# Attention over 32 groups of four heads: another order of the step, one call for the values, finished batches at fixed steps, and a prologue by batch

## What is computed

```python
def _L0_xattn_ref(x, ctx, pos_map, ctx_pos_map, Wq, Wkv, Wout, bout):   # 32 heads of 8, 256 keys
    q = (x @ Wq).reshape(b, n, N_HEADS, HEAD_DIM)
    k, v = jnp.split(ctx @ Wkv, 2, axis=-1)
    ...
    q = apply_axial_rope(q, pos_map)
    k = apply_axial_rope(k, ctx_pos_map)
    logits = jnp.einsum('bqhd,bkhd->bhqk', q, k) * scale
    w = jax.nn.softmax(logits, axis=-1)
    attn = jnp.einsum('bhqk,bkhd->bqhd', w, v)
    return attn.reshape(b, n, N_HEADS * HEAD_DIM) @ Wout + bout
x = x + jnp.tanh(g_xattn[0]) * _L0_xattn_ref(_layernorm(x, axis=-1), ctx_1024, ...)
x = x + jnp.tanh(g_ffn[0]) * _L0_ffn_ref(_layernorm(x, axis=-1), ...)   # 2 shared, 32 routed experts, top 6
```

## Time and profile before

| | us |
|---|---|
| median of three runs | 469.26 (468.69 to 469.92) |
| profiled execution | 466.33 |
| its span, first to last instruction | 464.5 |
| TensorE (PE) matmuls busy | 446.4 (96%) |
| VectorE (DVE) busy | 285.4 (61%) |
| ScalarE (ACT) busy | 198.8 (43%) |
| GpSimd (POOL) busy | 141.5 (30%) |
| first score matmul of the loop | at 37.75 |
| transposition with the maxima of the last group | at 178.14 |

### The profile page before, as it was taken

The page is one execution under the profiler, slowest core; times in us unless marked ns, Lnnn a source line. Parts: engine busy times, 40 slices in busy tenths (PEclk is TensorE's granted clock), DMA queues, the critical chain, the costliest instruction groups (busy, mean ns, idle before and its releaser), DMA issues.

```text
span 464.5 us, 8154 instructions
## 1 busy us (share of the span) xinstructions
PE 446.4 (96%) x2515; PEld 334.4 (72%) x2515; DVE 285.4 (61%) x579; ACT 198.8 (43%) x366; POOL 141.5 (30%) x229
## 2 busy tenths in 40 slices
PE   5888999999999998999999999999999999999996
PEld 5556666666666665676887888888888888888885
DVE  7798877777777674554427555554445555544555
ACT  1487887777777655463213222222222222222221
POOL 9066700000000000334245443333444433344430
PEclk9899999999999999999999999999999999999999
DMA  8201111111111000956998332324332233333102
GB/s 225 61 9 50 35 30 33 35 33 33 31 33 36 25 1 0 325 176 176 313 303 210 93 90 90 90 93 115 103 96 91 90 90 90 98 114 104 46 0 92
DMA packets 34056, 43.62 MB, mean 94 GB/s; under 512 B 5633, under 2 KB 28209, under 8 KB 34033
## 3 DMA queue, kind: packets, MB, share of 16 engines
q1 hardware_dynamic: 30737, 42.07, 31.5%
q10 hardware_dynamic: 3296, 1.25, 1.2%
HBM read 37.93 MB, written 1.18 MB: 84 GB/s over the span
## 4 chain that ended last, share of the span: by engine, by line
PE 86%; DVE 5%; DMA 3%; ACT 2%; issue 1%; SPq 1%; POOL 0%; DVEq 0%; ACTq 0%
PE psum L1159 26%; PE psum L1142 25%; PE psum L993 8%; PE psum L1006 7%; PE psum L969 6%; PE psum L956 3%; PE psum L980 2%; DMA G<-gates_by_expert 2%; PE psum L1055 2%; PE psum L912 2%; PE psum L884 1%; PE psum L921 1%; DVE nmax L735 1%; PE psum L1017 1%; SPq L307 1%
## 5 line engine op out<-in xcount | busy, mean ns | idle before, releaser
L608 ACT ACTIVATE hh<-hu 128x512 fp32r<-128x512 f32 x88 | 55.6, 633 | 186.9 <-DVE hu L853 186.9
L853 DVE SCALAR_TENSOR_TENSOR hu<-psum,b1cols,G 128x512 f32<-128x512 f32 x88 | 65.8, 750 | 109.3 <-PE psum L1142 98.9
L735 DVE TENSOR_REDUCE nmax<-psum 128x2 f32<-128x512 f32 x128 | 85.1, 687 | 26.0 <-PE psum L969 24.5
L499 ACT ACTIVATE probs<-psum 128x512 f32<-128x512 f32 x128 | 69.4, 595 | 14.1 <-PE psum L993 13.7
L1159 PE MATMUL psum<-hh,w2h 128*128 128x512 f32 (+1 forms) x188 | 73.5, 391 | 0.4 <-POOL hl L384 0.3
L1159 PE MATMUL psum<-hh,w2l 128*128 128x512 f32 (+1 forms) x188 | 73.2, 389 | 0.0
L1159 PE MATMUL psum<-hl,w2h 128*128 128x512 f32 (+1 forms) x188 | 73.2, 389 | 0.0
L859 DVE SCALAR_TENSOR_TENSOR hl<-hu,hh 128x512 fp32r<-128x512 f32 x88 | 61.4, 700 | 9.6 <-ACT hh L608 9.6
L1142 PE MATMUL psum<-xTh,w1h 128*128 128x512 f32 (+1 forms) x188 | 58.2, 391 | 0.0
L415 POOL CAST w2h<-w 128x256 fp32r x44 | 18.4, 417 | 130.2 <-PE psum L1159 130.2
L1142 PE MATMUL psum<-xTl,w1h 128*128 128x512 f32 (+1 forms) x188 | 57.9, 389 | 0.0
(11 more groups left out here) (150 smaller groups left out, 540.5 us busy)
## 6 DMA issues: line engine op xcount, KB each, us to landing
G<-gates_by_expert SPq DMA_DIRECT2D x40, 256.0 KB, 3.9
w<-in_L_ffn_rw_dram SPq DMA_DIRECT2D x4, 1408.0 KB, 11.9
w<-in_L_ffn_rw_dram SPq DMA_DIRECT2D x2, 2816.0 KB, 17.1
G<-gates_by_expert SPq DMA_DIRECT2D x8, 448.0 KB, 3.6
Kd<-QK SPq DMA_DIRECT2D x104, 32.0 KB, 1.8
G<-gates_by_expert SPq DMA_DIRECT2D x8, 384.0 KB, 3.5
G<-gates_by_expert SPq DMA_DIRECT2D x8, 320.0 KB, 3.7
G<-gates_by_expert SPq DMA_DIRECT2D x8, 192.0 KB, 3.8
```

Source lines behind the costliest of these rows:

```text
L499: act.activation(probs[g % 2][:, kt, 2 * hp:2 * hp + 2, :], ST_BANK[(4 * g + n) % 3][:, :].rearrange("p (h q) -> p h q", h=2), ACT.Exp, sc ...
L608: act.activation(hh[(SHT + j) % 2][:, cols], hu[2 * j + half][:, :], ACT.Relu).then_inc(rhh_ok, 1)
L735: dve.tensor_reduce(nmax[i % 2][:, qt, 2 * hp:2 * hp + 2], S_BANK[n % 2][:, :].rearrange("p (h k) -> p h k", h=2), AX.X, ALU.max, negate=T ...
L853: dve.scalar_tensor_tensor(out=hu[2 * (j % 2) + half][:, :], in0=H_BANK[2 * (j % 2) + half], scalar=b1cols[:, bass.ds(it * len(G) + j, 1)] ...
```

## The change

The loop's step has another order: scores 2, transposition with the maxima, scores 3, values of both halves in one call, finished batches, outputs, score 0 of the next group, shifted scores 0 and 1, next score 1, shifted 2, transposes of the group four ahead, shifted 3. On ScalarE the four exponentials come last in a step; several waits go, since others imply them. Finished batches are handled in fixed steps: transposed in 11, 19 and 27, projected and added in 12, 20 and 28; the copies of the transposed attention go to two tiles of Vx (0 and 3). In the prologue context and rows are loaded and transposed by batch, the statistics of the first two batches go ahead of the others, ScalarE normalises the rows and clears four of the five key buffers, the angle chain on VectorE uses operations with two tensor inputs (against tiles of constants), and the square root is a power of -0.5 on GpSimd, with the Newton step behind it as before. `WARM_UP` and `WARM_START` are 7 and 2 instead of 14 and 8. The shared experts' weights are loaded from SP's queue.

The diff, cut to what the prediction speaks of:

```diff
-WARM_UP, WARM_START = 14, 8
+WARM_UP, WARM_START = 7, 2
...
-        ATTN_STEPS = [GROUPS - 5, GROUPS - 3, GROUPS - 1]
-        PROJ_STEPS = [GROUPS - 4, GROUPS - 2, GROUPS - 1]
-        RESIDUAL_STEPS = [GROUPS - 4, GROUPS - 2, GROUPS - 1]
+        ATTN_STEPS = [NG * (b + 1) + 3 for b in range(B - 1)]
+        PROJ_STEPS = [n + 1 for n in ATTN_STEPS]
+        RESIDUAL_STEPS = PROJ_STEPS
...
+            load_context(0)
+            load_rows(0)
+            sp.dma_start(wkv_sb[:, :], wkv).then_inc(wkv_ld, 16)
+            load_context(1)
+            load_rows(1)
             sp.dma_start(wq_sb[:, :, :], wq.rearrange("(k p) n -> p k n", p=P)).then_inc(wq_ld, 16)
-            sp.dma_start(wkv_sb[:, :], wkv).then_inc(wkv_ld, 16)
+            load_context(2)
+            load_context(3)
+            load_rows(2)
+            load_rows(3)
...
-            for i in range(RING - 1):
-                last = pool.memset(Kd[i][:, :, :].bitcast(F32), 0.0)
-            last.then_inc(kd_clear, 1)
+            then(pool.memset(halves[:, :], -0.5))
+
+            def inverse_root(n, tiles):
+                pool.wait_ge(var_ok, n)
+                pool.tensor_tensor(rough[:, tiles], veps[:, tiles], halves[:, tiles], ALU.pow).then_inc(root_ok, 1)
...
+            def clear_keys(i):
+                if i == 0:
+                    act.wait_ge(consts_ok, 1)
+                act.activation(Kd[i][:, :, :], consts[:, 0, 0:1].unsqueeze(2).to_broadcast([P, GH, N]), ACT.Copy).then_inc(kd_clear, 1)
...
-            square_root(1, slice(0, NT))
-
+            clear_keys(0)
+            clear_keys(1)
+            context(0)
+            context(1)
+            act.wait_ge(ang_ok, 1)
+            act.activation(trig[:, :, :, :], ang[:, :, :].rearrange("p s (t f) -> p s t f", f=4), ACT.Sin).then_inc(trig_ok, 1)
...
+            act.wait_ge(rstd_ok, 1)
+            normalise_rows(0, xn[:, 0], xn_ok)
             read_values(0)
+            evacuate(0)
+            context(2)
+            context(3)
+            act.wait_ge(rstd_ok, 2)
+            normalise_rows(1, xn[:, 1], xn_ok)
             read_values(1)
-            evacuate(0)
             evacuate(1)
-
-            for k in range(KD):
-                act.dma_start(w1s[:, k, :].rearrange("p (e h) -> p e h", h=HID),
-                              sw1.rearrange("e (k p) h -> p k e h", p=P)[:, k]).then_inc(ws_ld, 16)
-            sflat2 = sw2.rearrange("e h n -> (e h) n")
-            act.dma_start(w2s[:, 0:SFULL, :], sflat2[0:SFULL * P, :].rearrange("(t p) n -> p t n", p=P)).then_inc(ws_ld, 16)
-            act.dma_start(w2s[0:SREST, SFULL, :], sflat2[SFULL * P:NS * HID, :]).then_inc(ws_ld, 16)
+            clear_keys(2)
+            clear_keys(3)
...
+                if b + 2 < B:
+                    act.wait_ge(rstd_ok, 3)
+                    normalise_rows(b + 2, xn[:, b + 2], xn_ok)
...
-                    exponentials(g, 0)
-                    exponentials(g, 1)
                 p = (i - 3) // 2
                 if i % 2 and 0 <= p < PAIRS:
-                    act.wait_ge(pv_mm, 2 * (i - 1))
-                    if p >= 2:
-                        act.wait_ge(ot_mm, p - 1)
+                    act.wait_ge(pv_mm, i - 1)
                     act.activation(oT[p % 2][:, :], O_BANK[:, 0:N], ACT.Copy).then_inc(o_ok, 1)
-                if i in ATTN_STEPS[1:]:
+                if i in ATTN_STEPS:
                     transposed_attention(ATTN_STEPS.index(i))
                 if 0 <= g < GROUPS:
-                    exponentials(g, 2)
-                    exponentials(g, 3)
-                if i == ATTN_STEPS[0]:
-                    transposed_attention(0)
...
-            square_root(2, slice(0, NT - TB))
...
-            square_root(3, slice(NT - TB, NT))
...
-            dve.tensor_scalar(sine[:, :, :, 0], pos_sb[:, :, :], 1.0, None, ALU.mult)
-            then(dve.tensor_scalar(sine[:, :, :, 1], pos_sb[:, :, :], FREQ1, None, ALU.mult))
-            then(dve.tensor_scalar(ang[:, 1], ang[:, 0], float(np.pi / 2), None, ALU.add))
-            then(dve.tensor_scalar(turns[:, :, :], ang[:, :, :], float(1 / TWO_PI), ROUND, ALU.mult, ALU.add))
-            then(dve.tensor_scalar(turns[:, :, :], turns[:, :, :], ROUND, None, ALU.subtract))
+            zeros = consts[:, 0].rearrange("p (t a f) -> p t a f", t=NT, a=2)
+            both = [consts[:, n].rearrange("p (s t) -> p s t", s=2) for n in range(4)]
+            for f, factor in enumerate((1.0, FREQ1)):
+                ins = dve.scalar_tensor_tensor(out=sine[:, :, :, f], in0=pos_sb[:, :, :], scalar=factor,
+                                               in1=zeros[:, :, :, f], op0=ALU.mult, op1=ALU.add)
+            then(ins)
+            then(dve.scalar_tensor_tensor(out=ang[:, 1], in0=ang[:, 0], scalar=float(np.pi / 2), in1=both[0][:, 0],
+                                          op0=ALU.add, op1=ALU.add))
+            then(dve.scalar_tensor_tensor(out=turns[:, :, :], in0=ang[:, :, :], scalar=float(1 / TWO_PI), in1=both[1],
+                                          op0=ALU.mult, op1=ALU.add))
...
-                then(dve.reciprocal(rstd[:, rows], root[:, rows]))
-                then(dve.tensor_tensor(newton[:, rows], rstd[:, rows], rstd[:, rows], ALU.mult))
+                then(dve.tensor_tensor(newton[:, rows], rough[:, rows], rough[:, rows], ALU.mult))
...
-            inverse_deviations(0, NT)
-            for b in range(B):
-                normalise_rows(b, xn[:, b], xn_ok)
+            row_variances(0, TB)
+            row_variances(TB, TB)
+            row_scales(0, TB)
+            row_scales(TB, TB)
...
                 multiply_turns(b, 1, A_KV[b % 2][:, :, 0:D])
+                if b == 0:
+                    row_variances(2 * TB, 2 * TB)
+                    add_turns(b, 1)
                 dve.wait_ge(q_mm, b + 1)
                 multiply_turns(b, 0, A_Q[b % 2].rearrange("p (t n) -> p t n", t=TB))
+                if b == 0:
+                    row_scales(2 * TB, 2 * TB)
+                if b:
+                    add_turns(b, 1)
+                add_turns(b, 0)
                 if b == B - 1:
 
                     dve.wait_ge(b1_mm, 1)
                     dve.tensor_copy(b1cols[:, :], A_B1[:, 0:TILES]).then_inc(b1_ok, 1)
                     dve.tensor_scalar(b1half[:, :], A_B1[:, SB_ROW:TILES], 1.0 / NS, None, ALU.mult).then_inc(b1_ok, 1)
-                add_turns(b, 1)
-                add_turns(b, 0)
 
 
             def row_max(i, n):
...
-                dve.tensor_copy(dst[:, :, :, R_MAX], nmax[g % 2][:, :, :]).then_inc(mhi_ok, 1)
+                dve.tensor_tensor(dst[:, :, :, R_MAX], nmax[g % 2][:, :, :],
+                                  consts[:, 0, 0:TB * GH].rearrange("p (t h) -> p t h", t=TB), ALU.add).then_inc(mhi_ok, 1)
...
+                    row_max(i, 3)
+                    maxima(i)
                 if i >= 4 and i % 2 == 0:
                     normalise((i - 4) // 2)
-                if i < GROUPS:
-                    row_max(i, 3)
-                    maxima(i)
                 if i in RESIDUAL_STEPS:
                     residual(RESIDUAL_STEPS.index(i))
...
-            def values(i, kt):
+            def values(i):
 
 
                 b, g = i // NG, i % NG
-                pe.wait_ge(exp_ok, 4 * i + 2 * (kt + 1))
                 second = i % 2
-                if kt == 0 and not second and i:
-                    pe.wait_ge(o_ok, i // 2)
-                for h in range(GH):
-                    ins = pe.matmul(O_BANK[HR * h:HR * h + HR, 0:N], Vx[:, TB * b + kt, GH * g + h, :], probs[i % 2][:, kt, h, :],
-                                    start=(kt == 0 and not second), stop=(kt == TB - 1 and bool(second)),
-                                    skip_group_check=True)
+                for kt in range(TB):
+                    pe.wait_ge(exp_ok, 4 * i + 2 * (kt + 1))
+                    for h in range(GH):
+                        ins = pe.matmul(O_BANK[HR * h:HR * h + HR, 0:N], Vx[:, TB * b + kt, GH * g + h, :], probs[i % 2][:, kt, h, :],
+                                        start=(kt == 0 and not second), stop=(kt == TB - 1 and bool(second)),
+                                        skip_group_check=True)
                 ins.then_inc(pv_mm, 1)
...
+                    keys_copied(0)
                     scores(i, 0)
                     scores(i, 1)
-                if weighted:
-                    values(i - 2, 0)
+                    transposes(AHEAD)
+                    keys_copied(1)
+                if new:
+                    scores(i, 2)
                 if shifted:
                     transposed_with_max(i - 1)
-                if i + AHEAD < GROUPS:
-                    transposes(i + AHEAD)
-                elif i == ATTN_STEPS[1]:
-                    attention_transposed(1)
-                elif i == PROJ_STEPS[1]:
-                    output_projection(1)
-                elif i == ATTN_STEPS[2]:
-                    attention_transposed(2)
                 if new:
```

(27 more changed lines are left out.)

167 lines of the change are left out of this document (103 added, 64 removed).

## The result

The changed kernel takes 456.94 us (median, 456.44 to 457.92), the kernel before 469.25 (468.69 to 469.92): a ratio of 0.9742, 95% interval 0.9723 to 0.9761. 456.2 was forecast. Its profiled run took 456.51 us with a span of 454.7.

A forecast was written before the change was run, and what follows sets the result against it. TensorE was taken to bound the loop, VectorE the part before it. Prologue -6.0, loop -7.0 and tail -0.1 sum to -13.1 us: 453.2 from the profiled run, 456.2 against the median; range 449 to 464.5.

The forecast's parts named there:

- Angle chain, first scores: Prologue: angle chain ends at 6.2 instead of 11.6, first scores move from 37.75 to about 31.8, -6.0 us.
- The power on GpSimd: Prologue and tail: taken at 0.3 us, replacing a square root and reciprocal; over 1 us was a sign of being wrong.
- Steady step: Attention loop: one visit fewer takes TensorE's step from 4.18 to 3.83 us, with bounds 3.77 and 4.1.
- The price of a visit: Attention loop, TensorE: going to the 32-column shape and back costs 0.3 us; two a step become one.
- QT's wait: Attention step, TensorE: 0.06 us lost before the shifted scores, which wait for QT; forecast to go.
- Finished batches: Steps 11-12, 19-20, 27-28: transposes, projection and residual cost 3.9 us each, 11.7 for three, VectorE waits included.
- case 4: Rival, more than forecast: batches cost only TensorE's 2.5 us each, or VectorE's other pre-loop waits go too: 450; chance 0.14.
- Tail: After the loop: values' new place +0.3 us, an exponential table load gone; -0.1 us in all.
- From the profiled run to the median: Whole kernel: 453.2 us from the profiled run; the old median's 2.9 above its profiled run carried over, giving 456.2.
- 1: Rival, loop gives nothing: ScalarE's ring or VectorE's maxima set the step at 4.05 us; time 463.1, chance 0.2.
- 3: Rival, slower: ScalarE's exponentials without overlap make the step 4.5 us on the mean; time 477 us, chance 0.04.
- 2: Rival, prologue gives little (-3 us), since ScalarE took over 7.5 us of clears and normalisations: time 459.2, chance 0.12.

The follow-up runs named there:

- e7: Changed kernel with the four key buffers cleared by GpSimd again, ahead of its halves and first powers, not by ScalarE: 3.7 us more than the changed kernel.
- e4: Changed kernel with the old numbers of warm-up transposes, 14 and 8 in place of 7 and 2: 458.61 us.
- e9: e8 with TensorE's wait for the second group's copied keys moved from ahead of the first group's third scores to behind its fourth: 453.81 us.
- e15: e9 with ScalarE's two gate activations and the table load ahead of them moved behind the last high parts of the prologue: 455.20 us.
- e1: Changed kernel with a group's values in two calls again, the second after the next group's first scores: 468.56 us.
- e5: Kernel before, with the first half of the values moved right ahead of the second half, in the old order of the step: 468.68 us.
- e8: Changed kernel with VectorE's residual ahead of the normalisation and a batch's two statistics behind the next group's first two row maxima: 453.00 us.
- e6: Changed kernel with both the old one-input angle chain and the key-buffer clears on GpSimd: 7.1 us more than the changed kernel.
- e2: Changed kernel with the old angle chain of one-input operations in place of two-input ones: 2.7 us more than the changed kernel.
- e14: e5 with the next group's first scores also moved ahead of the last shifted pair, parting the two score matmuls: 471.44 us.
- e3: Changed kernel with the finished batches at steps 26, 28 and 30 in place of 11, 19 and 27: 454.60 us.

## Why the prediction was right

The time is 0.7 us from the forecast. The parts, as forecast and as the profile has them:

- **Angle chain, first scores.** 6.2 forecast, 5.67 measured; 31.8 and 31.51, so -6.24 for -6.0. Right in sum, with two terms wrong. The power on GpSimd took 0.71 us at 2 elements and 1.12 at 4, not 0.3. The second is over the 1 us that I had named as a sign of being wrong; in the prologue it cost nothing, since VectorE had other work until each result was there (only in e7 did it wait for one, 2.51 us); in the tail VectorE waits 0.82 us for the last one, and TensorE, busy with warm-ups there, goes from the last projection to the experts in 6.99 us as before. And I had costed the halved first warm-up at nothing: e4 shows that with 14 of them the first multiplication comes 1.7 us later. I had the multiplication at 11.9; it came at 10.58, and VectorE's work behind it took longer, since two sums of 0.42 took 0.81 and 1.49 beside GpSimd's low parts. One error hides the other.
- **Start of the loop.** The sum went from the first scores straight to the first QT transposition as if the 3.81 us between them stayed. They became 5.43, +1.62. Two terms were missing. Since ScalarE's table load and high parts hadn't moved forward as far as the scores, GpSimd's last low part ends 4.21 us behind them, not 3.52, and VectorE's writing of the maxima ends with it: +0.69. And the new order sets a score of the next group ahead of that transposition, which waits for its bank until 36.61: QT starts 1.22 behind the low part's end, before 0.29: +0.93. The wait for the copied keys (0.73) isn't the cause, for e9 moved it and QT came no earlier; with the low part out of the way too, e15 has 4.49 in place of 5.43.
- **Steady step.** 3.83 forecast, 3.82 measured, 4.05 for the rival. The price of a visit, 0.3 us, was right (e1: 0.335), and TensorE is busy throughout. But the reason given for the step is half of it. Had only the call been merged, the old order would have kept the time (e5); with only the order changed, it would have as well (e1). I had named QT's wait as going with the new order, at 0.06 us; it would have been 0.11 to 0.34.
- **Finished batches.** 3.9 forecast, 3.57 measured; e8 removes two waits and is left with 2.4 to 2.5, my floor for case 4. The split into 2.4 of TensorE's and 1.6 of waits was near (2.5 and 1.1). From the first to the last transposition: 129.6 forecast, 128.25 measured.
- **Tail.** -0.1 forecast. From the last transposition to the experts' first output matmul it was +0.8 (24.62 for 23.79), of which 0.5 come with the values' new place, forecast as 0.3; behind the stall of the earlier trace rows, which is gone, +0.2 are left. In the expert part, which I had left alone, 2.9 us were lost: 1.4 for the gates' transfer, and about 1.5 for the fall of the clock at 208.8. The two aren't independent: e9, which has no fall there, stalls for 1.90 us and is 1.1 us shorter. The wait for the gates is a term that was missing. The fall I could not have placed: the changed kernel's profiled run has it, that of the kernel before doesn't.
- **From the profiled run to the median.** Here the prediction was lucky. The sum was -13.1 and the profiled runs differ by 9.8. The median of the kernel before stands 2.9 us above its profiled run and I carried that over; that of the changed kernel stands 0.4 above its own. What the sum missed (+1.6, +1.4, +1.5) was given back by the loop (1.3) and by these 2.5 us.

Of the rivals, 1 and 3 fall by the step of 3.82, and 2 by the scores at 31.51: ScalarE did not set the prologue, but e7 shows that its taking over the clears was worth 3.7 us.

## What to carry to other kernels

Price an edit by what it takes off the bound engine, then check in the new order that every consumer still has cover: merging the calls was worth 0.8 us by the medians (0.17%, not to be told from none; 2.4 us of the profiled loop) in one order and 11 in the other. When a first stage is pulled forward, go through all that was placed to fit the old start (warm-ups, waits for copies, table loads), since each is a new bound within a microsecond or two. And in an engine that runs in order, put bookkeeping behind the results that others wait for: a few lines moved were worth 3.9 us here. Before a shorter wait in one profile is put down to an edit, look whether the clock fell ahead of it: here a stall of 1.4 us vanished behind such a fall, and the time stayed the same.

## What the runs showed of the chip

- A power of two SBUF operands on GpSimd takes 0.71 us for 2 elements a lane, 0.70 in its second row and 1.12 for 4.
- VectorE's one-input operations on SBUF ended with GpSimd's memset in e6 and e2 alike, also at 16 elements. In the kernel before the first ones got through at the end of one memset (0.80 to 0.90 us); in e6 one was held over four in a row (3.18 us). Two-input ones took 0.23 beside a memset (and the changed kernel's chain). The other way round, two-input operations of VectorE were held beside GpSimd's two-input ones: 1.13 us in place of 0.17, and 1.49 in place of 0.42.
- TensorE's granted clock falls to half (1.2 GHz) for 3.4 or 6.8 us, in a few places and not in every run. In the prologue it fell in the six profiles in which TensorE had stood idle for 2.3 to 4.9 us on end (before, e5, e14, e2, e7, e6), and in none of the eight where the longest such idle was 1.8. At the start of the loop it fell in five (e1, e3, e4, e7, e9), behind several short waits that the others have too. In the expert part it fell in eight during, or up to 0.7 us behind, eight matmuls that read 34 partitions in place of 128, with TensorE busy all the time, and in four (e4, e6, e7, e15) 1.0 to 1.2 us behind the stall for the gates; in the kernel before and e9 not at all. In the changed kernel's TensorE these matmuls are, 0.6 us ahead of the fall at 208.8:

```profile
204.50 3.70 PE L1265 MATMUL psum<-gTf,b_sb 34*128 34x512 f32 x8
```

- In the profiled runs of the order before, the part from the last QT transposition to the end took 286.4 us with no fall in it, 287.9 with 3.4 us (e14) and 289.6 with 6.8 (e5): some 1.6 us for each 3.4. A kernel whose few runs hold different numbers of such stretches differs from itself by some 2 us, so smaller differences were read here from the steps of the profile. No run was made to find out what sets the falls off.
